# Masked attention, first key block: the mask by VectorE in place of a TensorE product, and maxima taken off by rows of -1

## The reference, cut to what matters

```python
Q, K, V = (proj(q, w_q), proj(k, w_k), proj(v, w_v))        # 4 batches x 16 heads, 16 wide
scores = jnp.einsum('bhqd,bhkd->bhqk', Q, K) / jnp.sqrt(jnp.float32(dk))
scores = jnp.where(mask == 0, NEG, scores)                  # mask 512 x 512, one for all heads
attn = jax.nn.softmax(scores, axis=-1)
out = jnp.einsum('bhqk,bhkd->bhqd', attn, V)
```

## Time and profile before

| | us |
|---|---|
| runs | 1209.94, 1201.06, 1202.81; median 1202.81 |
| the profiled execution | 1203.75 |
| its span, first to last instruction | 1202.0 |
| masked attention's first product to its last step's, in the span | 793.0 to 1078.4 |
| busy in the span: TensorE, VectorE, ScalarE, GpSimd | 1050.5, 659.1, 636.5, 200.0 |

### The profile page before, as it was taken

How to read it: one execution, slowest core, us unless ns; L and a number is a source line. 1 busy time by engine, 2 the same in 40 slices (tenths; PEclk the granted TensorE clock), 3 DMA queues, 4 the chain that set the end, 5 groups by cost and what they waited for, 6 DMA issues and landing times. The chain is left out here.

```text
span 1202.0 us, 21977 instructions
## 1 busy us (share of the span) xinstructions
PE 1050.5 (87%) x6945; PEld 658.6 (55%) x6979; DVE 659.1 (55%) x1993; ACT 636.5 (53%) x1275; POOL 200.0 (17%) x466
## 2 busy tenths in 40 slices
PE   7999999999978698999999991648999999987487
PEld 5555555655545498999999981213333333325254
DVE  4427888888856611211111104857666666775697
ACT  2447877877633232333333321526777777763697
POOL 0000000000000122222222210012222222330222
PEclk9958999999999898999999995869999999998798
DMA  5087898888749336666666644443111111100001
GB/s 184 1 306 293 321 330 322 316 321 324 290 141 360 136 110 226 223 222 219 225 218 222 220 140 153 152 147 91 47 49 46 47 46 46 47 20 10 0 32 40
DMA packets 75342, 199.55 MB, mean 166 GB/s; under 512 B 7880, under 2 KB 40904, under 8 KB 69256
## 3 DMA queue, kind: packets, MB, share of 16 engines
q1 hardware_dynamic: 71528, 188.45, 46.1%
q0 software_dynamic: 3744, 10.23, 2.2%
HBM read 134.82 MB, written 63.83 MB: 165 GB/s over the span
## 5 line engine op out<-in xcount | busy, mean ns | idle before, releaser
L784 DVE CUSTOM_DVE_ANT_0 unused<-mpsS,mask_bias 128x512 bf16<-128x512 f32 x256 | 172.0, 691 | 83.3 <-PE mpsS L717 82.9
L1526 ACT ACTIVATE hT<-ph,w 128x128 f32<-128x128 f32 x312 | 89.2, 369 | 207.7 <-PE ph L1500 207.7
L811 ACT ACTIVATE mPT<-mpsB 128x512 f32<-128x512 f32 x256 | 152.7, 597 | 81.1 <-PE mpsB L724 67.1
L1500 PE MATMUL ph<-xT,w 128*128 128x128 f32 x1248 | 152.1, 282 | 7.5 <-DMA w<-in_w1p 7.1
L1500 PEld LDWEIGHTS ph<-xT,w 128*128 128x128 f32 x1248 | 147.3, 197 | 10.8 <-issue 10.5
L1545 DVE TENSOR_TENSOR xn<-py,b 128x256 f32<-128x256 f32 x39 | 16.6, 425 | 247.4 <-PE py L1510 247.4
L1510 PE MATMUL py<-w,hT 128*128 x624 | 141.2, 379 | 0.7 <-DVE xn L1545 0.7
L659 ACT ACTIVATE scores<-scores,nm 128x512 f32<-128x512 f32 (+3 forms) x256 | 125.6, 557 | 9.8 <-DVE nm L624 9.8
L1510 PEld LDWEIGHTS py<-w,hT 128*128 128x128 f32 x624 | 115.6, 190 | 15.2 <-issue 1.1
L717 PE MATMUL mpsS<-mqk 96*128 96x512 bf16 x256 | 101.2, 397 | 19.5 <-DMA mqk<-packed 15.7
L611 DVE CUSTOM_DVE_ANT_0 scores<-psS,bias 128x512 f32<-128x512 f32 (+3 forms) x176 | 77.8, 487 | 54.6 <-PE psS L552 38.2
(11 more groups left out here) (267 smaller groups left out, 1621.5 us busy)
## 6 DMA issues: line engine op xcount, KB each, us to landing
w<-in_w1p SPq DMA_DIRECT2D x39, 1028.0 KB, 5.8
rel<-stage SPq DMA_DIRECT2D x44, 640.0 KB, 4.6
bias<-rel SPq DMA_DIRECT2D x44, 640.0 KB, 7.1
x<-rel SPq DMA_DIRECT2D x20, 640.0 KB, 6.8
mqk<-packed SPq DMA_DIRECT2D x64, 192.0 KB
w<-in_w2p SPq DMA_DIRECT2D x8, 1024.0 KB, 12.7
rel<-x SPq DMA_DIRECT2D x10, 640.0 KB, 3.2
rel<-mask_bias SPq DMA_DIRECT2D x10, 640.0 KB, 5.0
```

The lines of the kernel that those rows point to most:

```text
L784: nc.vector.tensor_tensor_reduce(out=unused[:, i, :], in0=psS[i % 2][:, :], in1=mask_bias[:, i, :], scale=1.0, scalar=-3.0e38, op0=ALU.add ...
L811: nc.scalar.activation(PT[r][:, j, :], psB[j % 2][:, :], ACT.Exp, scale=1.0 / 4).then_inc(s_exp, 1)
L1500: mm = nc.tensor.matmul(ph[half][:, q * P:(q + 1) * P], w1[i][:, dk * F + f * P:dk * F + (f + 1) * P], xT[i][:, dk, :], start=(dk == 0), s ...
L1526: g = nc.scalar.activation(hT[i][:, f, :], ph[half][:, q * P:(q + 1) * P], ACT.Gelu, bias=w1[i][:, DK * F + f:DK * F + f + 1])
```

## The change

For the first key block (i = 0) of each head, TensorE no longer issues the mask product: L722 alone closes the bank. VectorE adds the block of the turned mask to that bank and writes the sum to a new buffer `masked0` in SBUF, and ScalarE takes this block's exponential from there. The add stands in VectorE's queue behind the first L784 of the step and ahead of the second. ScalarE goes through the blocks in the order 1, 0, 2, 3. The bank of block 0 is free for block 2 when the add has read it (`s_added`), so L722 of block 2 now waits for the add; the other counts of `s_exp` follow the new order. The key half of the three rows holds -1.0, so the maxima themselves are split and GpSimd's negation falls away (four instructions a head in place of five). The diff:

```diff
--- before.py
+++ after.py
@@ -674,7 +674,7 @@
                 PT = [sb(ctx, f"mPT{r}", [P, NI, S]) for r in range(ROUND)]
                 unused = sb(ctx, "unused", [P, NI, S], BF16)
                 mx = sb(ctx, "mmx", [P, RING, NI])
-                neg = sb(ctx, "mneg", [P, RING, NI])
+                masked0 = sb(ctx, "masked0", [P, S])
                 zero = sb(ctx, "mzero", [P, NI])
                 rest = sb(ctx, "mrest", [P, RING, NI])
                 mp = sb(ctx, "mpieces", [P, RING, NI, 4], BF16)
@@ -684,9 +684,9 @@
                 psB = banks(ctx, "mpsB", 2)
                 psM = ctx.enter_context(nc.psum_tensor("mpsM", [P, 1024], BF16))
                 s_qk = [sem(f"s_mqk{r}") for r in range(RING)]
-                names = ("one", "smm", "soft", "mp", "mt", "row", "bmm", "exp", "seen")
+                names = ("one", "smm", "soft", "mp", "mt", "row", "bmm", "exp", "seen", "added")
                 s_seen_p = sem("s_mseenp")
-                s_one, s_smm, s_soft, s_mp, s_mt, s_row, s_bmm, s_exp, s_seen = (sem(f"s_m{n}") for n in names)
+                s_one, s_smm, s_soft, s_mp, s_mt, s_row, s_bmm, s_exp, s_seen, s_added = (sem(f"s_m{n}") for n in names)
                 block = ctx.enter_context(nc.Block())
 
                 @block.sync
@@ -718,14 +718,18 @@
                                                  start=True, stop=True).then_inc(s_smm, 1)
                             if late:
                                 m, slot, turn = late
-                                wait(pe, s_exp, NI * m + i - 1)
-                                nc.tensor.matmul(psB[i % 2][:, :], qk[slot][:, S + i * P:S + (i + 1) * P], qk[slot][:, 0:S],
-                                                 start=True, stop=False)
-                                nc.tensor.matmul(psB[i % 2][:, :], identb[:, :], maskT[:, i, :],
-                                                 start=False, stop=True).then_inc(s_bmm, 1)
+                                if i == 2:
+                                    pe.wait_ge(s_added, m + 1)
+                                else:
+                                    wait(pe, s_exp, NI * m + (-1, 0, None, 1)[i])
+                                mm = nc.tensor.matmul(psB[i % 2][:, :], qk[slot][:, S + i * P:S + (i + 1) * P], qk[slot][:, 0:S],
+                                                      start=True, stop=(i == 0))
+                                if i > 0:
+                                    mm = nc.tensor.matmul(psB[i % 2][:, :], identb[:, :], maskT[:, i, :], start=False, stop=True)
+                                mm.then_inc(s_bmm, 1)
                             if rows and i == 1:
                                 m, slot, turn = rows
-                                pe.wait_ge(s_mp, 5 * (m + 1))
+                                pe.wait_ge(s_mp, 4 * (m + 1))
                                 wait(pe, s_row, m)
                                 for k in range(NI):
                                     tr = nc.tensor.transpose(psM[KP:KP + 3, k * P:(k + 1) * P], mp[:, slot, k, 0:3], identb[:, :])
@@ -753,37 +757,42 @@
 
                             pool.wait_ge(s_soft, NI * (m + 1))
                             wait(pool, s_mt, m - RING + 1)
-                            wait(pool, s_mp, 5 * m)
+                            wait(pool, s_mp, 4 * m)
                             pool.sem_inc(s_seen_p, 1)
-                            nc.gpsimd.tensor_scalar(neg[:, slot, :], mx[:, slot, :], -1.0, 0.0, ALU.mult, ALU.add).then_inc(s_mp, 1)
-                            pool.wait_ge(s_mp, 5 * m + 1)
-                            nc.gpsimd.tensor_tensor(mp[:, slot, :, 0], neg[:, slot, :], zero[:, :], ALU.add).then_inc(s_mp, 1)
-                            pool.wait_ge(s_mp, 5 * m + 2)
-                            nc.gpsimd.tensor_tensor(rest[:, slot, :], neg[:, slot, :], mp[:, slot, :, 0], ALU.subtract).then_inc(s_mp, 1)
-                            pool.wait_ge(s_mp, 5 * m + 3)
+                            nc.gpsimd.tensor_tensor(mp[:, slot, :, 0], mx[:, slot, :], zero[:, :], ALU.add).then_inc(s_mp, 1)
+                            pool.wait_ge(s_mp, 4 * m + 1)
+                            nc.gpsimd.tensor_tensor(rest[:, slot, :], mx[:, slot, :], mp[:, slot, :, 0], ALU.subtract).then_inc(s_mp, 1)
+                            pool.wait_ge(s_mp, 4 * m + 2)
                             nc.gpsimd.tensor_tensor(mp[:, slot, :, 1], rest[:, slot, :], zero[:, :], ALU.add).then_inc(s_mp, 1)
-                            pool.wait_ge(s_mp, 5 * m + 4)
+                            pool.wait_ge(s_mp, 4 * m + 3)
                             nc.gpsimd.tensor_tensor(mp[:, slot, :, 2], rest[:, slot, :], mp[:, slot, :, 1], ALU.subtract).then_inc(s_mp, 1)
                     run_heads(pool, -LOAD, NBH - 1, step)
 
                 @block.vector
                 def _(dve):
                     for r in range(RING):
-                        nc.vector.memset(qk[r][KP:KM, S:2 * S], 1.0).then_inc(s_one, 1)
+                        nc.vector.memset(qk[r][KP:KM, S:2 * S], -1.0).then_inc(s_one, 1)
                     nc.vector.memset(zero[:, :], 0.0).then_inc(s_one, 1)
                     vals.clear(dve)
                     weights.clear(dve)
 
                     def step(n, r, it):
                         if h := stage_of(n, r, it, SOFT):
-                            m, slot, turn = h
-                            wait(dve, s_soft, NI * m)
-                            for i in range(NI):
+                            wait(dve, s_soft, NI * h[0])
+                        late = stage_of(n, r, it, 0)
+                        for i in range(NI):
+                            if h:
+                                m, slot, turn = h
                                 dve.wait_ge(s_smm, NI * m + i + 1)
                                 dve.sem_inc(s_seen, 1)
                                 nc.vector.tensor_tensor_reduce(
                                     out=unused[:, i, :], in0=psS[i % 2][:, :], in1=mask_bias[:, i, :], scale=1.0, scalar=-3.0e38,
                                     op0=ALU.add, op1=ALU.max, accum_out=mx[:, slot, i:i + 1]).then_inc(s_soft, 1)
+                            if late and i == 0:
+                                m = late[0]
+                                dve.wait_ge(s_bmm, NI * m + 1)
+                                wait(dve, s_exp, NI * m - 2)
+                                nc.vector.tensor_tensor(masked0[:, :], psB[0][:, :], maskT[:, 0, :], ALU.add).then_inc(s_added, 1)
                         if r % GROUP == 2 and (h := group_of(n, r, it, 2)):
                             vals.divide(dve, *h)
 
@@ -804,11 +813,15 @@
                         if late and r % GROUP == 0:
                             g, par = group_of(n, r, it, 0)
                             wait(act, vals.s_pv, NI * (g - 1))
-                        for j in range(NI):
+                        for j in (1, 0, 2, 3):
                             if late:
                                 m, slot, turn = late
-                                act.wait_ge(s_bmm, NI * m + j + 1)
-                                nc.scalar.activation(PT[r][:, j, :], psB[j % 2][:, :], ACT.Exp, scale=1.0 / 4).then_inc(s_exp, 1)
+                                if j == 0:
+                                    act.wait_ge(s_added, m + 1)
+                                else:
+                                    act.wait_ge(s_bmm, NI * m + j + 1)
+                                nc.scalar.activation(PT[r][:, j, :], masked0[:, :] if j == 0 else psB[j % 2][:, :], ACT.Exp,
+                                                     scale=1.0 / 4).then_inc(s_exp, 1)
                             if rows and j == 2:
                                 m, slot, turn = rows
                                 act.wait_ge(s_mt, m + 1)
```

## The result

The changed kernel takes 1212.68 us in the median of six runs (1208.69 to 1214.84), the kernel before 1202.88 us beside it: 1.0063 times the time, with a 95% interval of 1.0039 to 1.0087. It is slower, by less than 1%. A second set of runs on another occasion gave 1.0070 (1.0047 to 1.0092). The forecast was 1211.6 us, with a range of 1203 to 1220 us.

A forecast was written before the change was run, and what follows sets the result against it. TensorE's queue was taken to bound the kernel, then VectorE's add to delay it: +8.3, -0.9, +1.7 and -0.3 make +8.8 us on 1203.75, 1212.5, less 0.94 for the median: 1211.6 us, range 1203 to 1220 us.

The forecast's parts named there:

- T: Time from a step's first L717 (block 0) to its last (block 3): 2.38 us before, 2.545 us forecast.
- rival 1: TensorE stays the bound in the masked stage: 13.8 us go, 1189 us; chance 0.10.
- rival 2: VectorE's instructions don't overlap around the add: T 2.69 us, +17.3 us, 1220 us; chance 0.17.
- rival 3: The add hands over in 0.45 to 0.5 us, gain and loss cancel: T 2.4 us, 1201 to 1206 us; chance 0.10.
- What bounds: TensorE's queue sets the masked stage's pace; one product less saves 0.215 us a step if nothing is late.
- The chain: From a step's first L717 through L784, add and second L784 to block 3's L717: 2.545 us, 0.165 us later.
- The other wait: L722 of block 2 waits some 0.2 us for the add, its product going at 1.93 us instead of 1.72.
- steps 7 to 56: 50 plain steps of the masked stage, each 0.165 us longer: +8.3 us.
- the stage's start to the end of step 3: Steps 0 to 3: TensorE, partly at half clock, remains the bound and gains from the missing product and negation: -0.9 us.
- steps 4 to 6: Behind L1653, VectorE starts late and then runs without a gap; T sums to 10.5 us from 8.8: +1.7 us.
- steps 57 to 61: In three of them GpSimd is held up and transposes come late, T about 2.7 us: together -0.3 us.
- the fear of the prediction's last paragraph: TensorE's clock falling in the new pauses of the masked stage would show the forecast wrong; no size given.

The follow-up runs named there:

- the add alone: The changed kernel with the negation and the rows of 1.0 put back: 1.0065 times the kernel before, stage 305.7 us.
- the rows alone: The kernel before with the rows of -1 and without GpSimd's negation, nothing else: 0.9969 times the kernel before, stage 292.5 us.

## Why the prediction was right

It was right in direction, size and cause. Its rivals are out: T is 2.54 us and not 2.16 (rival 1) or 2.69 (rival 2, no overlap), and the second L784 starts 0.61 us behind the add, not 0.45 to 0.5 (rival 3).

- *What bounds.* The run without mask product and add gives 3.92 us a step where 4.13 - 0.215 was said.
- *The chain.* 0.57 + 0.61 + 0.60 + 0.69 + 0.06, taken as 2.545 us, measured 2.54. The add was priced from a row of another stage at 0.68 us and 0.60 us until the next instruction; it took 0.686 and 0.61. The two narrower adds and the later one show that it is this chain that holds TensorE, and each came within 0.03 us of its sum.
- *The other wait.* L722 of block 2, now L725, waits for the add as said, and it is inside the chain.
- *ScalarE.* Reading block 0 from SBUF costs 630 ns where 597 are read from PSUM. That was costed at nothing, and nothing depends on it. The order of the exponentials mattered more than the prediction said; the experiment prices it at 0.33 us a step.
- *GpSimd.* Hidden in plain steps, as said.

The sum, term by term, each from one profiled execution against that of the kernel before:

| term | said, us | changed, us | changed, second time, us |
|---|---|---|---|
| steps 7 to 56 | +8.3 | +8.0 | +7.9 |
| the stage's start to the end of step 3 | -0.9 | +0.2 | -1.2 |
| steps 4 to 6 | +1.7 | +2.2 | +1.8 |
| steps 57 to 61 | -0.3 | -0.5 | -0.5 |
| behind them, to the next stage | 0 | -1.2 | -1.1 |
| sum over the stage | +8.8 | +8.7 | +6.9 |

The large term is solid. That the sum in the first column of measurements meets the forecast within 0.1 us is luck: three small terms were off there and cancelled, and the second execution gives 6.9. Steps 4 to 6 have T of 3.84, 3.60 and 3.60 us, where 3.3, 3.61 and 3.61 were said (the first is 3.39 in the second execution). For the later two the timeline shows VectorE without a gap from one weight reduction to the next.

```profile
829.73 2.28 DVE L1666 TENSOR_REDUCE asum<-xnT 128x1 f32<-128x2048 f32 x1
...
830.29 0.39 PE L717 MATMUL mpsS<-mqk 96*128 96x512 bf16 x1
...
831.93 0.68 DVE L788 CUSTOM_DVE_ANT_0 unused<-mpsS,mask_bias 128x512 bf16<-128x512 f32 x1
...
833.89 0.39 PE L717 MATMUL mpsS<-mqk 96*128 96x512 bf16 x1
```

The end of the stage, costed at 0, gained 1.2 us. It is not the negation as such: the run with the add alone has the negation and gained 1.0 us there. In the changed kernel, with the rows alone and with the add alone GpSimd's last piece takes 0.20 or 0.21 us, where it takes 1.06 beside a weight instruction in the kernel before. Of steps 57 to 61 the prediction had GpSimd late in three; T in the kernel before is 2.89 to 2.97 us in four. In the first steps a gain of 0.7 us was there when step 2 began (18.17 us behind the first product against 18.86), and then TensorE's clock was at half for longer than before:

```profile
818.00:820.00 2.00, 1.94 (x5) 0.43 (x4) 0.73 (x4) 1.72 (x3) 0.41 (x3) 0.50 0.57 197
820.00:822.00 2.00, 2.00 (x9) 0.61 (x8) 1.91 (x5) 0.42 (x1) 0.40 (x2) 0.50 0.31 74
```

In both executions TensorE waits 1.95 us for a load there, and then the granted clock falls to 1.2 GHz; before it was back when step 3 began, here it was not until the end of it. In the second execution of the changed kernel the load wait is 1.50 us, the granted clock stays at 1.00 from 810 to 828 us, and step 7 is reached 1.9 us sooner (42.9 against 44.8). So the loss in these steps is one of that execution, and the second shows the gain that was forecast. Why the clock came back later in one than in the other is open.

One sign named in advance was wrong: the busy share of TensorE went from 99% to 96%, not to 90%. The profile counts a product of 512 columns as busy for 0.38 us while the next can follow 0.215 us behind, so 0.38 us of pauses in a step shows as less than half of that.

On the page of the Trainium skill that the prediction set against its sum ("VectorE: DVE Perf Modes", section "The DRAIN you can't avoid"): the prediction quoted only half of it. The same paragraph goes on: "A next op that is not held starts earlier" (what is held it leaves to another section), so the page doesn't make whole durations the rule for every instruction, as the prediction and its rival 2 had it. Here an instruction queued behind another that it doesn't depend on starts 0.07 to 0.08 us before that one's end, in front of the add and behind it. By whole durations T would have been 2.69 us; it is 2.54, and the measurement decides.

## What to carry to other kernels

Room in an engine's busy time doesn't say where in its queue a new instruction can stand: follow the banks that the instructions behind it are to free, and compare that chain with the bound engine's own time from the same starting point. A work item taken off the bound engine gains only until the first such chain, so put its replacement behind the last instruction whose result is wanted soon; here the same exchange on the last block, with two copies moved, turned a loss of 0.7% into a gain of 0.8%. When one engine gets faster, look at the order of the small copies on a third: they were hidden at 4.13 us a step and were not at 3.92.

## What the runs showed of the hardware

The exponential of 128 x 512 took 630 ns from SBUF and 597 ns from PSUM. A sum out of PSUM took 0.69, 0.42 and 0.28 us for 512, 256 and 128 columns, and what stood behind it started 0.61, 0.34 and 0.20 us behind its start. A GpSimd instruction on 128 x 4 that takes 0.21 us took 1.06 us when it started 0.32 us into one of VectorE's 1.32 us weight instructions; why was not tried. TensorE's clock stayed at 2.4 GHz through the two pauses in each step, about 0.21 us ahead of L725 of block 2 and 0.16 us ahead of L717 of block 3 (1.00 in all stretches of 20 us from 840 to 1100 us), so the fear of the prediction's last paragraph did not come true. The part of the program ahead of the stage varies by up to 9 us from run to run (789.9 to 798.7 us), as much as many of the differences measured here; the stage by itself is the better measure.
